# First chunk of a two-layer kernel: counts of two pieces turned by DMA, and GpSimd's rstd placed ahead of four bias additions

## What is computed

```python
xn = _layernorm(x)
s = einsum('bsk,nk->bsn', xn, masked_weight) + bias
inter = xn @ c1_w.T @ c2_w.T                      # rank 16, 1792 columns
idx = argmax(inter.reshape(rows, 56, 32), -1) + arange(0, 1792, 32)
h = relu(einsum('bkm,bm->bk', w1[idx], xn))       # one of each 32 columns
g = einsum('bk,bkm->bm', h, w2t[idx])
x = x + s * silu(g)
```

## Time and profile before

| | |
|---|---|
| median of 3 runs | 650.04 us |
| profiled execution, its own time | 650.05 us |
| span of its instructions | 648.2 us |
| granted TensorE clock | 0.999 of full speed |
| TensorE busy | 632.3 us (98%) |
| VectorE busy | 446.3 us (69%) |
| ScalarE busy | 213.4 us (33%) |
| GpSimd busy | 240.0 us (37%) |

### The profile page before, as it was taken

The page is one execution under the profiler, slowest core; times in us unless marked ns, Lnnn a source line. Parts: engine busy times, 40 slices in busy tenths (PEclk is TensorE's granted clock), DMA queues, the critical chain, the costliest instruction groups (busy, mean ns, idle before and its releaser), DMA issues.

```text
span 648.2 us, 8466 instructions
## 1 busy us (share of the span) xinstructions
PE 632.3 (98%) x2942; PEld 509.9 (79%) x2942; DVE 446.3 (69%) x716; ACT 213.4 (33%) x379; POOL 240.0 (37%) x188
## 2 busy tenths in 40 slices
PE   7999999999999999999999999999999999999997
PEld 3768787878888878888878787778878878887887
DVE  7987776787765777765777886655765857575633
ACT  3533333312223312223322243651255035314510
POOL 2355545650000740000742644582425433351441
PEclk9999999999999999999999999999999999999999
DMA  9940000022400022300153622050140013012000
GB/s 282 400 158 1 2 0 1 26 81 52 127 17 9 26 81 70 108 16 8 32 141 95 173 82 73 17 178 1 49 147 1 16 50 129 0 41 89 2 32 33
DMA packets 42575, 46.16 MB, mean 71 GB/s; under 512 B 25072, under 2 KB 25456, under 8 KB 41904
## 3 DMA queue, kind: packets, MB, share of 16 engines
q1 hardware_dynamic: 42544, 45.76, 22.1%
HBM read 31.85 MB, written 8.39 MB: 62 GB/s over the span
## 4 chain that ended last, share of the span: by engine, by line
PE 81%; DVE 12%; issue 3%; ACT 1%; POOL 1%; DMA 1%; DVEq 0%; POOLq 0%; ACTq 0%; SPq 0%
PE bank L418 73%; DVE counts L940 3%; PE bank L348 2%; DVE seg_top L926 2%; DVE eq L928 2%; PE bank L1205 1%; PE bank L1359 1%; DMA first<-counts 1%; PE bank L1183 1%; DVE h_lo L970 1%; PE bank L1322 1%; DVE h L961 1%; POOL g_tile L394 1%; PE bank L1224 1%; DVE ws_raw L994 0%
## 5 line engine op out<-in xcount | busy, mean ns | idle before, releaser
L418 PE MATMUL bank<-w_hi_t,h_hi 128*128 128x512 f32 x224 | 90.4, 404 | 0.7 <-DVE h_lo L970 0.4
L761 ACT ACTIVATE h_hi<-h 128x512 fp32r<-128x512 f32 x56 | 35.4, 633 | 162.9 <-DVE h L961 162.9
L418 PE MATMUL bank<-w_lo_t,h_hi 128*128 128x512 f32 x224 | 87.6, 391 | 0.0
L418 PE MATMUL bank<-xT_hi,w_hi_t 128*128 128x512 f32 x224 | 87.4, 390 | 0.1
L418 PE MATMUL bank<-w_hi_t,h_lo 128*128 128x512 f32 x224 | 87.4, 390 | 0.0
L418 PE MATMUL bank<-xT_hi,w_lo_t 128*128 128x512 f32 x224 | 87.2, 389 | 0.0
L418 PE MATMUL bank<-xT_lo,w_hi_t 128*128 128x512 f32 x224 | 87.1, 389 | 0.0
L940 DVE TENSOR_TENSOR_SCAN counts<-restart,eq 128x512 bf16<-128x512 bf16 (+1 forms) x56 | 76.0, 1357 | 2.4
L394 POOL TENSOR_TENSOR g_tile<-g_tile,s_tile 128x512 f32<-128x512 f32 x31 | 44.3, 1430 | 88.3 <-DVE g_tile L983 44.2
L926 DVE TENSOR_REDUCE seg_top<-bank 128x16 f32<-128x512 f32 (+1 forms) x64 | 39.5, 617 | 46.2 <-PE bank L1205 46.2
L672 POOL TENSOR_TENSOR prod_lo<-prod,prod_hi 128x512 fp32r<-128x512 f32 x32 | 40.6, 1291 | 57.9 <-ACT prod_hi L801 57.8
(11 more groups left out here) (191 smaller groups left out, 1300.5 us busy)
## 6 DMA issues: line engine op xcount, KB each, us to landing
w_raw<-in_w SPq DMA_DIRECT2D x28, 256.0 KB, 10.1
x_res<-in_x SPq DMA_DIRECT2D x4, 1024.0 KB, 8.5
mid_state<-g_tile SPq DMA_DIRECT2D x16, 256.0 KB, 2.1
x_tile<-mid_state SPq DMA_DIRECT2D x4, 1024.0 KB, 7.4
x_res<-mid_state SPq DMA_DIRECT2D x4, 1024.0 KB, 5.5
out<-g_tile SPq DMA_DIRECT2D x15, 256.0 KB, 2.0
x_tile<-in_x SPq DMA_DIRECT2D x3, 1024.0 KB, 5.6
b_raw<-in_lora_b SPq DMA_DIRECT2D x2, 1024.0 KB, 5.1
```

The source lines that it names most:

```text
L418: last = nc.tensor.matmul(dst, a, b, start=(start and n == 0), stop=(stop and n == len(mms) - 1))
L761: nc.scalar.activation(h_hi[:, it % 2, :], h[:], ACT.Copy).then_inc(h_hi_done, 1)
```

## The change

In the first chunk TensorE transposes only the counts of pieces 0 and 1 (tiles 0 to 7). Those of pieces 2 and 3 are scanned into `counts` and turned by eight DMA transposes that SyncE issues behind next_rows; those of piece 3 stand behind a wait for TensorE's last transposes, since they overwrite the counts of piece 1 in `first`. The scans of piece 3 wait until the turn of piece 2 for the same rows has landed. On GpSimd the rstd of chunk 1's rows is made ahead of head(0), and the first turn of its loop is written out.

```diff
+        BY_PE = 2
             for tt in range(TT):
-                sp.sem_inc(ld_first[tt], PIECES * 16)
+                sp.sem_inc(ld_first[tt], BY_PE * 16)
             next_rows(0, x_rows[1])
+            for p in range(BY_PE, PIECES):
+                if p % 2:
+                    sp.wait_ge(first_tr, 4 * BY_PE)
+                for tt in range(TT):
+                    turn(0, p, tt)
             rows_out(0, mid_rows[0], True)
...
             def body(c, last):
                 if last:
                     next_layer()
-                rows_rstd(gp, c + 1)
+                if not opens(c):
+                    rows_rstd(gp, c + 1)
...
+            rows_rstd(gp, 1)
             head(0)
-            with gp.Fori(0, CH - 1) as c:
+            body(0, False)
+            head(1)
+            with gp.Fori(1, CH - 1) as c:
                 body(c, False)
                 head(c + 1)
...
             def select_count(c, p, tt):
-                if not opens(c):
+                if not opens(c) or p > BY_PE:
                     dve.wait_ge(ld_first[tt], (c * PIECES + p) * 16)
                 elif tt == 0 and p >= 2:
                     dve.wait_ge(first_tr, 4 * (p - 1))
-                kept = first_counts[p % 2] if opens(c) else counts
+                kept = first_counts[p] if opens(c) and p < BY_PE else counts
...
                     dve.wait_ge(relu_done, c * IT + it + 1)
-                    if opens(c):
+                    if opens(c) and it < 4 * BY_PE:
                         dve.wait_ge(first_tr, it + 1)
                         which = first_bank
...
-                    if first:
+                    if first and it <= 4 * BY_PE:
                         first_transpose(it - 1)
```

## The result

The changed kernel takes 651.1 us (median of 22 runs, 650.58 to 653.35), the kernel before 649.38 us in the 22 runs beside it (649.10 to 651.43). The ratio is 1.0026, with a 95% interval of 1.0020 to 1.0032: 1.7 us slower, which is just above the 0.2% that a measurement of this kernel can tell. The profiled execution took 651.23 us with a span of 649.4 us and a granted clock of 0.999, as before.

The account below looks back on a forecast made before the run. TensorE was taken to bound the kernel, carrying 81% of the chain of waits. Its -2.17 us was not had because VectorE, sharing turns with GpSimd, sets the first chunk's end: +0.5 on 650.04, forecast 650.5 us, range 648.5 to 651.6.

Parts of the forecast that it names:

- Part 1: First chunk, tiles 8 to 13: six sets of four transposes leave TensorE; upper bound -2.17 us.
- Part 2: Eight DMA transposes on SyncE: cost 0, closest landing, tile 12's, hidden by 0.7 us; bounds nothing and 3.8 us.
- Part 3: End of first chunk: VectorE's masks with SBUF operands and normalisations take turns with GpSimd; VectorE sets the end, +0.5 us.
- the layout: Part 3's timetable of VectorE, ScalarE and GpSimd at the first chunk's end, last normalisation ending at 112.0 us.
- Part 4: GpSimd, first chunk: rstd ahead of the head's bias additions is worth 0.75 us, normalisations ending at 112.0 instead of 112.75.
- the race in the next head: Head of chunk 1: first scan loses to GpSimd's third gate, margin 0.10 us; +1.1 us, 651.6; chance 0.12.
- The reverse tip in the later head: One chunk later the first scan beats the gate it had lost to; -1.1 us, to 649.4; chance 0.04.
- The milder contention: First chunk: VectorE keeps up and TensorE decides, -2.17 in full, 647.9; normalisations alone free, 648.6; chance 0.18.
- a mask late by up to 3.8 us: First chunk: a turn of piece 3 lands late and delays tile 12's mask; 653 or 654 us; chance 0.03.
- The sum: -2.17 us for TensorE's path if VectorE kept up; VectorE does not and sets the chunk's end: +0.5 us.

Follow-up runs that it names:

- experiment 3: The changed kernel with one more wait on GpSimd, so the four bias additions start behind the normalisations: 649.31 us, ratio 0.9983 to the kernel before.
- experiment 11: The changed kernel with GpSimd's bias additions behind the normalisations in its loop too, no empty increments on SyncE: 646.95 us, ratio 0.9950 to the kernel before.
- experiment 10: The changed kernel with bias additions behind the normalisations in GpSimd's loop too, and 96 empty increments on SyncE: 646.38 us, ratio 0.9943 to the kernel before.
- experiments 6 to 8: Empty semaphore increments on SyncE ahead of the new turns: 32, then 96 in experiment 3's kernel, 32 in the changed kernel: 649.30, 648.76, 650.94 us.
- experiment 1: The changed kernel without its GpSimd half, rstd back behind the four bias additions: 654.27 us, ratio 1.0062 to the kernel before.
- experiment 5: The kernel before with rstd first on GpSimd and bias additions behind the normalisations, no new DMA turns: 650.07 us, ratio 1.0002 to the kernel before.
- experiment 4: The changed kernel with bias_a and the four additions moved forward on GpSimd, behind the remainders of tiles 2 to 6: 651.71 us, ratio 1.0026.
- padded copy: The changed kernel with 32 empty semaphore increments on SyncE ahead of the eight new turns: 650.94 us, ratio 1.0019 to the kernel before.
- experiments 1 and 9: The second of these: the kernel before with bias additions behind the normalisations inside GpSimd's loop: 647.91 us, ratio 0.9965 to the kernel before.

## Why the prediction was right or wrong

The forecast was 650.5 us in a range of 648.5 to 651.6; the measured 651.1 is inside the range, 0.6 above the point. No change within 0.2% had the largest chance, 0.67; the outcome, slower by 0.26%, had 0.15. That the number came so close is in part luck: the forecast stood on 650.04 us, the median of three runs, and the 22 runs of the kernel before have 649.38. Against its own base the change was to cost 0.5 us, and it cost 1.7.

- **Part 1, the blocks on TensorE**: right. 5.67 instead of 5.90 us a block, and with the additions out of the way the stretch falls to 38.57 (experiment 3), where 37.82 was the bound.
- **Part 2, "Cost 0"**: this is the step that failed, and it was 0.16 + 0.50. The last landing was to be hidden by 0.7 us. It took 3.00 us instead of 2.3, and its scan ended 0.3 us later than laid out, so it became the last thing that tile 12's mask waited for, by 0.16 us; in experiment 11, where it took 2.96, the relu ends at 106.05 and the mask starts at 106.18, and the stretch is 0.08 longer than in experiment 10, where the chain doesn't pass through it. Why it took 3.0 was not isolated. The larger part is that the eight instructions moved a later turn to a place in SyncE's program where it is issued 0.43 us late and lands 0.50 us late (experiments 6 to 8, 11). No term of the sum held that: the prediction asked what is queued behind the new turns in time, rightly found nothing, and didn't think of the program's length.
- **Part 3, masks and normalisations**: right in mechanism and size. Masks 0.83 to 1.71 us where 0.67 was free, h_lo 1.00, normalisations 3.83 us in all (laid out: from 108.3 to 112.0, 3.7), TensorE waiting 1.16 and 1.03 where 1.2 and 1.2 had been given. What the layout missed was small: with the profile's start (0.53 later) taken off, the scan was asked for at 101.81 and not 101.6, tile 11's h_lo ended 0.1 later than laid out, and tile 12's h_lo 0.3. The Trainium skill's "SBUF — State Buffer", section "Who interferes with whom", has the rule by which the masks go: a VectorE instruction with two SBUF inputs contends with a GpSimd one that reads SBUF. The masks agree with it: those of tiles 0 to 7, with a PSUM operand, stay at 0.66 to 0.69 us, and that of tile 12, with two SBUF operands, goes from 0.83 to 0.69 when the additions leave (experiment 3). Two rows are not covered by that sentence of the Trainium skill: the normalisations, which read one 512-wide tensor from SBUF, were held as well (3.83 against 1.92 us in experiment 3), and h_lo, with two SBUF inputs, was not held by GpSimd's pow (0.69 us across it).
- **Part 4, the worth of the rstd move**: right, with a reason that was incomplete. 0.75 was forecast; experiment 1 measured 2.2 us, of which 1.5 are TensorE's lower clock after its longer wait, and 0.7 the order on GpSimd. The prediction had no term for the clock. It compared the ends of the last normalisations (112.75 and 112.0); in the traces these lie 0.89 us apart, counted from the block of tile 6 (114.12 - 78.98 = 35.14 and 112.92 - 78.67 = 34.25). TensorE waits for the first: it starts on it 112.89 - 78.98 = 33.91 us into the stretch in experiment 1 and 110.73 - 78.67 = 32.06 with the change, 1.85 apart. Most of that lead is lost again with the change, where TensorE then waits a second time, 1.03 us for xT_lo. None of it enters the sum, which held only the new order.
- **The rivals**: the race in the next head was not lost. GpSimd's first gate stood 0.06 us later behind the rank product, and its third, which races the first scan, 0.14 us later; it started 0.25 us behind the scan where it had been 0.10, so the shift went away from the tip. The head lost 0.14 us to its second scan, not 1.1. The reverse tip in the later head was seen in this profile (-0.87), and both outcomes occur in traces without the new turns (24.49 before, 23.60 in experiment 5) and with them (24.51 in experiment 3, 23.62 here), so it is not counted as part of the difference; how often each comes in either kernel isn't known. The milder contention did not come. Nor did a mask late by up to 3.8 us; a landing of 3.00 us did, on the edge of its cover.
- **The sum**: +0.5 forecast. By the trace: +0.81 in the stretch, +0.50 for the late turn, +0.14 for the scans, 1.45 us. The ratio gives 1.7. The remaining 0.2 to 0.3 is within the interval (0.0020 to 0.0032 of 650 us is 1.3 to 2.1 us).

## What to carry to other kernels

Before work is taken off the engine that bounds, lay out the engine that is second in line, with the instructions that share its memory operands: here a PSUM operand that became an SBUF operand turned a free 0.67 us mask into one of up to 1.7 us. One wait that put GpSimd's less urgent work behind VectorE's urgent work freed the end of the chunk, though not the masks of tiles 8 to 10, which stand beside the weights' remainders (1.7 us in experiment 3 too). GpSimd's idle time is no room for such work; room is where VectorE has slack as well (experiment 4). Where an engine's program gets longer, compare the issue times of its later transfers too, since they can move by 0.5 us with nothing queued ahead of them. And before a difference is put down to a wait, look at the granted clock of the matmuls behind it (experiment 1).

## What the runs showed of the hardware

- Turns between VectorE and GpSimd cost VectorE up to one GpSimd pass each: masks of 1.71 us where 0.67 is free, with GpSimd passes beside them that take 1.29 us when alone and were recorded with 1.5 to 1.7 us. GpSimd's pow on the 128x4 values of rstd does not count in this: in the kernel before h_lo took 0.69 us across a pow of 1.02 us.
- Where an instruction stands in SyncE's program can delay it: 0.43 us at the issue and 0.50 us at the landing for a DMA transpose whose operand was ready, gone with 32 or 96 empty increments ahead of it and back without them. Which places are hit, and whether other engines have it, is open.
- The landing of a DMA transpose of 128x512 or 128x256 bf16 from SBUF to SBUF took 2.3 us at the median, and 3.0 to 3.1 for the last one of the first chunk in the changed kernel, its padded copy and experiment 11 (3.00, 3.08, 2.96). The cause is open.
- TensorE's granted clock fell to 0.50, the lower of its two levels (1.2 GHz), after it had stood idle for 2.97 us in experiment 1, and stayed there for about 3.4 us (113.85 to 117.24); twelve matmuls took 4.34 us instead of 2.83. At the start of the program it fell after 1.95 us without work in experiments 1 and 9, and not after 1.92 us in the kernel before, so the idle time alone does not tell.
- The block of tile 0 starts from 42.02 to 44.71 us in the traces of twelve kernels whose programs begin alike. In the five that start it at 42.86 or later (experiments 1 and 6 to 9) the clock was at half for a part of the time between 10 and 18 us; in the seven others (42.02 to 42.55) it was not. Whether the clock alone makes the difference is open. It is more than this change, and only stretches between two places of one trace show through it.
